# Attention's context tiles split first and transposed by DMA instead of TensorE, and the first head group's operands placed ahead of the last layer-norm tiles

## What is computed

```python
x = x + 0.5 * ffn(layernorm(x))                  # W1, W3: 1792 x 512, W2: 512 x 1792
qkv = layernorm(x) @ w_qkv.T + b_qkv             # 32 query heads, 8 key/value heads, 16 wide
q, k = rope(q), rope(k)
probs = softmax(where(causal, q @ k.T / 16, -max))
ctx = (probs @ v).reshape(B, S, 512)
x = x + ctx @ w_dense.T + b_dense
x = x + 0.5 * ffn(layernorm(x))
```

## Time and profile before

| what | value |
|---|---|
| median of 3 runs (lowest, highest) | 1449.14 us (1448.33, 1449.30) |
| the profiled execution's own time | 1450.07 us |
| its span in the trace | 1448.4 us |
| PE busy | 1374.4 us, 95% of the span |
| DVE busy | 1066.3 us, 74% |
| ACT, POOL busy | 608.2 us (42%), 182.7 us (13%) |
| granted TensorE clock, mean | 0.987 |

### The profile page before, as it was taken

One profiled execution on the slowest core, in us unless ns is written; L12 is line 12 of the kernel. 1 busy time (PEld: TensorE's weight loads), 2 busy tenths in 40 slices (PEclk: granted clock), 3 DMA queues, 4 the chain that ended last, 5 costly groups with the idle time before them and its releaser, 6 DMA issues.

```text
span 1448.4 us, 25511 instructions
## 1 busy us (share of the span) xinstructions
PE 1374.4 (95%) x9984; PEld 706.9 (49%) x9984; DVE 1066.3 (74%) x1611; ACT 608.2 (42%) x802; POOL 182.7 (13%) x269
## 2 busy tenths in 40 slices
PE   1999999999999978799999999999999999999998
PEld 0444444444444433233333333333577777777775
DVE  7999566764665578899999999965576666665544
ACT  4862222222211243378787777765222222222121
POOL 0000000000000354133323222211011011011000
PEclk9999999999999999699999999999999999999999
DMA  9703941011021021111111111030635646566540
GB/s 386 256 0 108 258 133 58 26 57 48 31 46 40 1 59 30 52 28 28 26 36 27 28 26 38 2 132 1 182 116 173 215 168 220 159 226 182 197 160 30
DMA packets 152028, 144.40 MB, mean 100 GB/s; under 512 B 129904, under 2 KB 133488, under 8 KB 148080
## 3 DMA queue, kind: packets, MB, share of 16 engines
q1 hardware_dynamic: 151920, 142.91, 31.4%
HBM read 96.73 MB, written 21.76 MB: 82 GB/s over the span
## 4 chain that ended last, share of the span: by engine, by line
PE 77%; DVE 13%; SPq 3%; issue 3%; ACT 3%; DMA 1%; POOL 0%; ACTq 0%; DVEq 0%
PE ps L2271 17%; PE ps L1819 15%; PE ps L2288 10%; PE ps L2045 9%; PE ps L1946 6%; PE ps L1840 6%; PE ps L2026 4%; PE ps L1866 3%; PE ps L2143 2%; PE ps L1936 2%; SPq L528 2%; SPq L532 2%; DVE rowmax L1552 1%; DVE w_raw L1167 1%; PE ps L2055 1%
## 5 line engine op out<-in xcount | busy, mean ns | idle before, releaser
L983 ACT ACTIVATE probs<-ps 128x1024 f32<-128x1024 f32 (+3 forms) x384 | 292.5, 812 | 83.9 <-PE ps L2026 82.3
L1819 PE MATMUL ps<-xt_hi,w_all 128*128 128x512 f16 x896 | 275.9, 382 | 16.2 <-DVE w_all L1207 16.0
L2271 PE MATMUL ps<-xs,wpair 128*128 128x256 f16 x2352 | 261.3, 273 | 0.9 <-DVE second_sum L1704 0.9
L2271 PEld LDWEIGHTS ps<-xs,wpair 128*128 128x128 f16 x2352 | 229.9, 98 | 33.7 <-DVE second_sum L1704 1.1
L1552 DVE TENSOR_REDUCE rowmax<-ps 128x2 f32<-128x1024 f32 (+3 forms) x208 | 237.3, 1141 | 9.0 <-PE ps L1954 3.8
L1946 PE MATMUL ps<-ka,qa 48*128 48x512 f16 (+3 forms) x768 | 159.7, 342 | 22.3 <-DVE rowmax L1552 9.5
L1819 PE MATMUL ps<-xt_lo,w_all 128*128 128x512 f16 x448 | 171.1, 382 | 0.0
L2045 PE MATMUL ps<-probs,vs 128*32 128x512 f32 (+3 forms) x1536 | 164.5, 500 | 2.4 <-ACT ctx_sb L1002 2.4
L1819 PEld LDWEIGHTS ps<-xt_hi,w_all 128*128 (+1 forms) x896 | 88.0, 98 | 124.9 <-issue 18.6
L1556 DVE TENSOR_REDUCE rowmax<-ps 128x1 f32<-128x512 f32 x192 | 131.1, 683 | 9.8 <-PE ps L1946 9.8
L2288 PE MATMUL ps<-wpair,hs_hi 128*128 128x512 f16 x448 | 133.4, 380 | 0.5 <-DVE hs_lo L1731 0.5
(11 more groups left out here) (168 smaller groups left out, 1818.1 us busy)
## 6 DMA issues: line engine op xcount, KB each, us to landing
wpair<-spill SPq DMA_DIRECT2D x28, 2304.0 KB, 8.9
spill<-block_parts SPq DMA_DIRECT2D x14, 512.0 KB, 2.7
spill<-w_all SPq DMA_DIRECT2D x24, 224.0 KB, 4.0
x<-x_in SPq DMA_DIRECT2D x4, 1024.0 KB, 5.5
wbase<-m1t SPq DMA_DIRECT2D x4, 896.0 KB, 12.4
w_raw<-w1t SPq DMA_DIRECT2D x4, 896.0 KB, 13.9
wbase<-m3t SPq DMA_DIRECT2D x4, 896.0 KB, 24.0
w_raw<-w3t SPq DMA_DIRECT2D x4, 896.0 KB, 24.2
```

Source lines behind the costliest of these rows:

```text
L983: nc.scalar.activation(probs[u % PBUF][:, 2 * pair:2 * pair + 2, 0:q1 - q0], wide(("scores", g, (u, pair)))[:, :, 0:q1 - q0], ACT.Exp, sca ...
L1819: last = mm(ps[:, bank, :], w[a][:, k, bass.ts(t, P)], xt[b][:, k, :], start=(k == 0 and n == 0), stop=(k == HB - 1 and n == 2))
L2271: last = mm(product_bank(n, i)[:, m, :], weight_of(n, m, a, weight, k), xs[c % 2][:, b, 2 * rows_ + k, :], start=(k == 0 and q == 0), stop ...
```

## The change

Two edits. First, in SP's QKV queue all of `place_first(2)` to `place_first(7)` stand ahead of `place_normal_tile(7, 2)` and `(7, 3)`. Second, the context tiles are no longer transposed by PE: DVE or ACT splits rows of `context` into `ctx_parts` (three buffers, fp16 high and low), and SP transposes both parts by DMA into `ctx_t` (four buffers where there were two). `transpose_rows` is gone from PE, `project` waits for the DMAs, and both splits of tiles 0 and 1 are made inside the last iteration of DVE's main loop. The loads of the first two weight pairs move from behind the loop to the end of iteration 14.

```diff
@@ SP, QKV
         place_first(1)
         place_normal_tile(7, 1)
-        place_first(2)
-        place_first(3)
+        for tt in range(2, SEQ_TILES):
+            place_first(tt)
         place_normal_tile(7, 2)
-        place_first(4)
         place_normal_tile(7, 3)
-        for tt in range(5, SEQ_TILES):
-            place_first(tt)
@@ SP, attention
+        def place_context(i):
+            sp.wait_ge(ctx_hi_ready, i + 1)
+            sp.wait_ge(ctx_lo_ready, i + 1)
+            if i >= 4:
+                sp.wait_ge(dense_full, i - 3)
+            for n in range(2):
+                sp.dma_start_transpose(ctx_t[i % 4][n][:, :, :], ctx_parts[i % 3][:, n, :]).then_inc(ctx_placed[i % 4], 16)
         for g in range(GROUPS):
+            if g == GROUPS - 1:
+                place_context(0)
+                place_context(1)
...
         sp.wait_ge(m_placed, 64 * GROUPS)
-        for v in range(BUF):
-            sp.wait_ge(qk_placed[v], placed(GROUPS - BUF + v))
-        load_pair(0)
-        load_pair(1)
+        for i in range(2, SEQ_TILES + 2):
+            place_context(i)
         sp.wait_ge(st_full, 2 * NU * (GROUPS - 2))
         place_rows(8, 0)
+        for i in range(SEQ_TILES + 2, SEQ_TILES + 5):
+            place_context(i)
         place_rows(8, 1)
+        for i in range(SEQ_TILES + 5, TOKEN_TILES):
+            place_context(i)
@@ ACT
         def context_high(i):
-            act.wait_ge(dt_full, i + 1)
-            act.wait_ge(dense_full, i - 1)
-            nc.scalar.copy(ctx_t[i % 2][0][:, :, :].rearrange("p a b -> p (a b)"), ps[:, rows_bank(i), :])\
+            context_ready(act, i)
+            ctx_parts_free(act, i)
+            nc.scalar.copy(ctx_parts[i % 3][:, 0, :].rearrange("p (a b) -> p a b", a=HB), context_rows(i))\
@@ DVE, main loop
             later_piece(k, 16)
+            if k == GROUPS - 1:
+                context_both(0)
...
             later_piece(k, 20)
+            if k == GROUPS - 1:
+                context_both(1)
@@ PE, project
             if q == 0:
-                pe.wait_ge(ctx_hi_ready, i + 1)
-                pe.wait_ge(ctx_lo_ready, i + 1)
+                pe.wait_ge(ctx_placed[i % 4], 32 * (i // 4 + 1))
+                if i == 0:
+                    pe.wait_ge(pair_taken, NPAIR * GROUPS)
+                elif i >= 2:
+                    pe.wait_ge(x2_ready, i - 1)
```

More of the change, by code:

```diff
@@ L385, in build, with ctx_parts_free, context_rows, context_ready @@
     LN_AT = {4: 4, 8: 5, 12: 6}
+    def ctx_parts_free(eng, i):
+        if i >= 3:
+            eng.wait_ge(ctx_placed[(i - 3) % 4], 32 * ((i - 3) // 4 + 1))
+    def context_rows(i):
+        return context[:, i % SEQ_TILES, :, i // SEQ_TILES, :]
+    def context_ready(eng, i):
+        b, tt = divmod(i, SEQ_TILES)
+        eng.wait_ge(single_taken, taken(("ctx", GROUPS * (b + 1) // BATCH - 1, tt // 4)))
     BLOCK_AT = {(1 if n < 8 else 2, 4 + n % 8): n for n in range(2 * HALF)}
@@ L584, in _ @@
                 place_operands(g + 3)
[L586 to L592, removed]
+            if g == GROUPS - 2:
+                sp.wait_ge(spilled, 16 * 28)
+                for i in range(2):
+                    sp.wait_ge(blocks_spilled[i], 16 * HALF)
+                for v in range(BUF):
+                    sp.wait_ge(qk_placed[v], placed(GROUPS - BUF + v))
+                load_pair(0)
+                load_pair(1)
         def place_rows(n, j):
@@ L1619, in later_piece, with context_high, context_low, context_both @@
                 reduce_piece(k, r)
+        def context_high(i):
+            context_ready(dve, i)
+            ctx_parts_free(dve, i)
+            nc.vector.tensor_copy(ctx_parts[i % 3][:, 0, :].rearrange("p (a b) -> p a b", a=HB), context_rows(i))\
+                .then_inc(ctx_hi_ready, 1)
+        def context_low(i):
+            dve.wait_ge(ctx_hi_ready, i + 1)
+            hi, lo = (ctx_parts[i % 3][:, n, :].rearrange("p (a b) -> p a b", a=HB) for n in range(2))
+            nc.vector.tensor_tensor(out=lo, in0=context_rows(i), in1=hi, op=ALU.subtract).then_inc(ctx_lo_ready, 1)
+        def context_both(i):
+            context_high(i)
+            context_low(i)
         for k in range(GROUPS):
@@ L1742, in second_pair, with add_and_sum @@
                 row_lo(9 + c, (p - 3) // 2)
[L1744 to L1747, removed]
-        dve.wait_ge(wd_unit, 1)
[L1749 to L1756, removed]
-        normalise(14, 0)
[L1758 to L1767, removed]
+        def add_and_sum(i):
+            add_dense(i)
+            if i < TPC:
+                dve.wait_ge(x2_ready, i + 1)
+                norm_rows(8, i)
+        context_both(2)
+        dve.wait_ge(wd_unit, 1)
+        add_and_sum(0)
+        context_both(3)
+        add_and_sum(1)
+        normalise(14, 0)
+        context_both(4)
+        add_and_sum(2)
+        context_both(5)
+        add_and_sum(3)
         normalise(14, 1)
-        context_high(5)
-        context_low(5)
+        context_both(6)
         add_dense(4)
@@ L1773, in _ @@
         norm_newton(8)
-        context_high(6)
-        context_low(6)
+        context_both(7)
         add_dense(5)
@@ L1784, in _ @@
         context_low(SEQ_TILES)
+        context_low(SEQ_TILES + 1)
         add_dense(7)
@@ L1787, in _ @@
         for i in range(SEQ_TILES, TOKEN_TILES):
-            if i + 1 < TOKEN_TILES:
-                context_low(i + 1)
+            if i + 2 < TOKEN_TILES:
+                context_low(i + 2)
             add_dense(i)
@@ L2122, in _ @@
             values(k - 1, 4)
[L2124 to L2132, removed]
-                last = tr(ps[:, rows_bank(i), q * P:(q + 1) * P], context[:, tt, q, b, :], ident[:, :])
-            last.then_inc(dt_full, 1)
         def project(i, q):
@@ L2244, in _ @@
         project(7, 1)
-        transpose_rows(8)
         project(7, 2)
@@ L2249, in _ @@
         for i in range(SEQ_TILES, TOKEN_TILES):
-            project(i, 0)
-            if i + 1 < TOKEN_TILES:
-                transpose_rows(i + 1)
-            for q in range(1, HB):
+            for q in range(HB):
                 project(i, q)
```

51 lines of the change are left out of this document (20 added, 31 removed).

## The result

Over 20 runs each, the changed kernel takes 1453.52 us (median) and the kernel before 1449.30; the ratio is 1.0022, with a 95% interval of 1.0013 to 1.0031. By the ratio that is some 3.2 us slower (1.9 to 4.5), by the medians 4.2. The interval is clear of 1, but the difference is about the 0.2% that the prediction took as the least that can be told from no change. The profiled execution took 1453.43 us, with a span of 1451.7. The prediction was 1451.4, with 1446.6 to 1454.6 as its range.

A forecast was written before the change was run, and what follows sets the result against it. PE, busy 95% of the span, was taken as the bound, with a chain of engines pacing tiles 8 to 15. Terms -1.4 + 1.9 - 4.9 + 3.9 + 2.8 = +2.3 gave 1451.4 us as a median, range 1446.6 to 1454.6.

The forecast's parts named there:

- QKV, -1.4: QKV stage: with chunk 7's transposes out of the way, PE's wait for group 0's operands shrinks by 1.4 us.
- I take it that 3.6 us of idling do the same as 5.0: QKV stage: the shortened wait still brings the clock down, losing 3.3 us as before; otherwise 3.3 us more are won.
- Splits in iteration 15, +1.9: Last attention iteration: two casts and two subtractions added to a full DVE cost 1.9 us, bounds 0 and 2.3.
- Transposes off PE, -4.9: Projection of tiles 0 to 7: PE saves its transposes and tile 0's wait, DMAs hidden; -4.9 us, bounds -5.2 and -4.0.
- The tail, +3.9: Tiles 8 to 15: PE waits 3.2, 3.45 and 5.0 us before tiles 8, 10 and 13; +3.9 us, bounds 0 and 6.5.
- The clock in the tail, +2.8: Tiles 8 to 15: half rate after idling is hidden before tile 8, unhidden before tile 13; +2.8 us, bounds 0 and 3.3.
- the rival: Tail: clock stays up before tile 8, falls before tiles 10 and 13, delaying the second xs pair 2.8; sum +5.1, chance 0.20.
- The sum would be the same, since the first two hide each other: Tail: even if all three gaps brought half rate, the clock's cost would stay the same.

The follow-up runs named there:

- the order alone: Kernel before with only the new order of SP's QKV queue; 1447.88 us, ratio to before 0.9986.
- the context part alone: Changed kernel with the old order of the QKV queue put back; 1456.08 us, ratio to before 1.0037.
- the first half alone: Changed kernel with context tiles 8 to 15 back on TensorE's transposes, tiles 0 to 7 still by DMA; 1445.07 us, ratio to before 0.9961.
- the pair moved behind: Changed kernel with the second xs pair behind all context tiles in SP's queue, not ahead of tile 13's; 1451.35 us, ratio to before 1.0012.
- filled waits: Changed kernel with unread products on TensorE in its waits before tiles 8, 10 and 13; 1450.82 us, ratio to before 1.0002.
- the order with its wait filled: Kernel before with the new QKV queue order and 20 unread products ahead of the first score piece; 1446.09 us, ratio to before 0.9967.
- the kernel with all three: Changed kernel with tiles 8 to 15 on TensorE's transposes, iteration 15's splits on GpSimd and the QKV wait filled; 1439.92 us, ratio to before 0.9924.

## Why the prediction was right

Its range held, and it named the mechanism: the places of all three waits, the clock's fall behind them, the loss in iteration 15 and the gain in the interleaved part. The time is 4.2 us more than before by the medians and 3.2 by the ratio, where 2.3 were forecast. Three terms were sized too small, one of them a gain.

- **QKV, -1.4.** The wait shrank by 1.46 and the piece starts 1.51 earlier, and the delayed transposes of chunk 7 cost nothing. But I took the stretch at 1.2 GHz to stay as long as it was; in this execution it was 3.3 us, and the end of iteration 14 came 3.6 us earlier, not 1.4 (3.0 of it by the end of group 0's row maxima; the other 0.6 arises in the loop and was not traced). The experiment with the order alone bounds the gain on average at 0.4 to 3.5. The step that was mis-sized is "I take it that 3.6 us of idling do the same as 5.0": they bring the clock down, but of the six profiled kernels with the new order and an unfilled wait, four then ran 3.3 us at half rate and two 6.6. The old order varies too: 6.5 us of work at half rate in the kernel before, some 4.6 in that with the context part alone. So it is not shown that the new order makes the stretch shorter.
- **Splits in iteration 15, +1.9.** 1.95 or 1.96 in each of the five kernels that have them there; shown to be VectorE's time by moving them to GpSimd.
- **Transposes off PE, -4.9.** -5.1, and again with the first half alone. PE has no wait for tiles 0 to 7: the cover held.
- **The tail, +3.9.** Without the clock it is 10.1 - 4.6 = 5.5. The wait before tile 8 is 3.26 against 3.2, the one before tile 10 2.49 against 3.45 (tile 8 ran slow ahead of it, for 1.8 us more), the one before tile 13 5.71 against 5.0. From there SP's queue was mis-sized: its first context transpose behind each xs pair takes 1.91 us, not 1.2, twice on the path, 1.4 us. I had used that SP is busy 1.2 us for each, from a place where nothing of 14 blocks was ahead; with the pair moved behind, tile 13's took 1.19. The rest is 0.2.
- **The clock in the tail, +2.8.** 4.6. It fell before all three tiles and not only once at a cost: the first fall is hidden as predicted, the last costs 2.96, and the one before tile 10 costs 1.7, for the reason that the rival gave: tile 10 runs slow, `add_dense(10)`, `row_lo(8, 1)` and the second xs pair come later, by the 1.7 us that the filled waits take back. "The sum would be the same, since the first two hide each other" was wrong: the first fall hides in the wait before tile 10, the second hides in nothing. The rival had it a full length, 5.1 in all, with the clock up before tile 8. In the changed kernel that condition was not met, and of its extra 2.8 us 1.7 came. In the kernel with the context part alone it was met (see the hardware section): from the first xs pair to the second it is 16.17 us (1014.41 to 1030.58), 2.6 more than with filled waits.

From the forecast's sum of +2.3 to the trace's +3.35: -2.2 in QKV, -0.2 in the interleaved part, +1.6 and +1.8 in the tail, and rounding. That the middle lay so close to the result is in part luck: the QKV term and the tail's were off by 2.2 and 3.4 us, in opposite directions.

What speaks against the change is not what the Trainium skill's prices ("VectorE: DVE Perf Modes", "The three transpose paths") would have it: eight blocks a tile were issued in 2.5 us and landed some 3.8 us after the first issue (1.24 to the second, 2.5 to its landing), well under half of the 10.5 us that the page's 1309 ns a block come to, as an estimate. What it costs is the latency, where a chain has nothing else to do.

## What to carry to other kernels

Here DMA transposes took work off a full TensorE at no price where something covered the 4 us from split to landing; where tiles follow each other in a chain, keep TensorE's transposes, four of which took 0.6 us. Decide it per tile, not per kernel: the same edit was worth -5 us in one half and +10 in the other. Put new work of a full loop on the engine that has a hole there, and count an idle stretch of TensorE at its length plus half of what may follow at 1.2 GHz; 13 to 24 products that nobody reads removed that part here, and cost nothing except where they outlasted the wait, by 0.9 us once.

## What the runs showed of the hardware

- The length of an idle stretch does not settle what the clock does. After 3.26 us of idling before tile 8 in the changed kernel PE ran at half rate for 3.6 us; in the kernel with the context part alone it idled 3.25 us at the same place and none followed, while 4.15 us before tile 10 brought it down. The windows of that kernel, over the idle time before tile 8, tile 8 and 9, the idle time before tile 10, and what follows:

```profile
1009.72:1012.97 3.25, 0.00 (x1) 0.01 (x1) 3.22 (x4) 0.01 (x1) 0.00 (x0) 1.00 0.40 81
1012.97:1018.30 5.33, 5.33 (x24) 2.17 (x24) 2.56 (x7) 1.24 (x2) 0.00 (x0) 1.00 0.81 155
1018.30:1022.48 4.18, 0.03 (x1) 0.00 (x0) 2.54 (x5) 1.68 (x1) 0.00 (x0) 0.86 0.77 148
1022.48:1028.40 5.92, 5.92 (x15) 2.19 (x16) 0.57 (x1) 1.85 (x3) 0.00 (x0) 0.52 0.44 89
```

  In that kernel the clock fell again before tile 13, after 5.45 us of idling. The rule of the Trainium skill, "TensorE: Matmul & The Clock Gate", section "Why this matters for your kernels", that a long idle gap between bursts of matmuls puts the engine back to half rate, holds here for most gaps of the tails, not for that one; and 2.49 us before tile 10 in the changed kernel were enough, where 1.96 before tile 13 with the xs pair moved and 1.65 before were not.
- The same wait of 3.56 us in QKV was followed by a half-rate stretch from 538.3 to 541.6 in the changed kernel, and in the kernel with filled waits, whose QKV part is the same program, by one from 536.4, still inside the wait, to 543.0:

```profile
536.40:543.00 6.60, 5.98 (x39) 2.88 (x40) 4.42 (x7) 2.45 (x4) 2.75 (x4) 0.50 0.39 80
```

  That is worth 1.5 us at the end of iteration 14, and a comparison of single traces carries it along.
- Every kernel here has another half-rate stretch at the start of the attention loop, where PE is idle a third of the time, 30 us long in the kernel before (576.2 to 606.5). In the profiled execution of the order with its wait filled it lasted until about 614. From the end of group 0's row maxima, at 581.8, to that of iteration 14 it took 350.0 us, and in the kernel with all three, from the same 581.8, 346.6; 3.4 of the difference is there by the end of iteration 3. That is nearly all of the 3.6 us by which this execution is above its median. Why it lasted longer stays open; no experiment was made on it.
- An xs pair (14 blocks each) ahead in SP's queue makes the next transpose of 4 blocks take 1.89 to 1.93 us instead of 1.2, in each of seven cases of four kernels.
